# Turning a block's routing weights by a VectorE transpose and four stores instead of TensorE and ScalarE

## The chip, the core and the metric

The kernel runs on one core of a Trainium2 chip. Its time is the device time of one launch in microseconds (us). Five engines work side by side and wait for each other by semaphores: TensorE (PE: matmuls, and transposes as matmuls with the identity), VectorE (DVE), ScalarE (ACT), GpSimd (POOL) and SyncE (SP), which only issues the transfers (DMAs) here. Each engine runs its own list of instructions strictly in order.

## The reference, cut to what matters

One pre-norm transformer block over x of 32 x 256 x 128 in fp32: windowed attention with 16 heads, then a mixture of 16 experts with a shared one. What the change touches is the routing of the second half: each token gets a weight for each expert (0 for all but four), and the experts' outputs are summed by these weights.

```python
    x = x + attn(layernorm(x), ...)
    h = layernorm(x)                                   # T = 8192 tokens of 128
    scores = sigmoid(h @ gate_w.T)                     # T x 16 experts
    # two best of four groups by their two best scores + bias, then four best experts in them
    topk_weight = scores of the four / (their sum + 1e-20) * 2.5
    inter = silu(h @ gate_proj.T) * (h @ up_proj.T)    # for each expert, 64 wide
    y = sum over the four experts of topk_weight * (inter @ down_proj.T)
    shared = silu(h @ sh_gate.T) * (h @ sh_up.T) @ sh_down.T
    return x + y + shared
```

## The kernel before

The 8192 tokens are 16 blocks (STEPS) of TOK = 512 tokens, four tiles of 128 (NT = 4). Stage 1 is the attention: one body for each block, up to about 380 us of the run. Stage 2, from 397 us on, is the expert half, 16 steps d = 0 to 15 of some 22 us. Between them lies a run-up (the functions called `last`), in which the last attention block is mixed with the turning of the expert weights and the routing of blocks 0 and 1.

A step of stage 2 has nine pairs of up and down (`up(d, p)`, `down(d, p)`, p = 0 to 8; eight pairs of experts and the shared expert). The experts are two to a matmul, 64 wide each, on the 128 partitions. For each p, PE computes the gate and up projections in three matmuls of 512 columns each (lines 1560 to 1562, the inputs split into a high and a low part), ACT takes the silu (L775), DVE multiplies (`gate(d, p)`, L1105), POOL multiplies by the routing weights (`weigh(d, p)`, L618), and PE projects down three places later (`down`, L1571; the shared expert's is L1574, with 64 rows in place of 128). `up(d, p)` waits for the gate of two places before.

`weigh` needs the weights of a block as `spread`: partition = one of 128 rows of an expert pair, columns = tokens, every expert's row of 512 weights repeated on 64 partitions. SP makes this by a trip through DRAM: `store_weight(d)` writes 16 rows of 512 weights to `wt_d` (weight_scratch), and `load_spread(d)` reads them with a broadcast, two loads of 1 MB. The two `spread` buffers are the `stacks` buffers of stage 1, so the profile calls them stacks.

The weights themselves come out with tokens on the partitions. DVE computes the routing of block d + 2 in step d, in pieces between its gates, and ends with `shares(d + 2)` ahead of `gate_shared(d)`. POOL multiplies (`scale_weight(d + 2)`, L608) into `weight`, [128, 4, 16]. In step d + 1 PE turns this by four transposes into PSUM (`transpose_weights`, L1548, after up(d, 2) and the shared down), ACT copies the result to `weightT`, [16, 512] (`take_weights`, L767), and SP stores it. For block 0 the same is done in the run-up, in turn with the transposes of the expert weights through the banks ps_max (the list WEIGHT_BANKS, lines 1491 and 740). Block 0's spread load can't leave before that.

The order on every engine is written out by hand in these functions. SP's order in a step is: load_x1(d + 4), load_residual(d), store_weight(d + 1), load_spread(d + 1), store_result(d - 1).

## Time and profile before

| | us |
|---|---|
| median of three runs | 761.34 (759.34 to 766.67) |
| the profiled execution | 758.62 |
| its span, first to last instruction | 756.8 |

| engine | busy us | share of the span |
|---|---|---|
| PE | 706.9 | 93% |
| DVE | 585.8 | 77% |
| ACT | 362.4 | 48% |
| POOL | 306.4 | 40% |

The mean granted TensorE clock is 0.972 of full speed, and 1.00 in stage 2. The chain of waits, followed back from the last instruction, lies on PE for 80% of the span, on DVE for 7% and in transfers for 5%. The shares are averages over both stages; what holds in a step of stage 2 is read from its windows and timelines. An instruction's row in a timeline gives its start, its length, its engine, its line and what it writes and reads; in brackets stands how long its engine was idle before it, and what ended that.

### The profile page before, as it was taken

The page shows a single profiled execution, that of the slowest core. Times are in us where ns is not written, and L with a number is a line of the kernel's source. Part 1 is how long each engine was busy: PE and PEld are TensorE (multiplying, and loading weights), DVE is VectorE, ACT ScalarE, POOL GpSimd, SP SyncE. Part 2 cuts the span into 40 slices and gives each one's busy share as a digit, 9 for nine tenths or more (in the row PEclk, how much of TensorE's full clock was granted, in tenths as well). Part 3 has the DMA queues.
Part 4 walks back from the last instruction along what each step waited for, and adds up shares of the span by engine and source line. Part 5 has one row for each costly group of instructions (what it writes and reads, how often), then busy time and mean ns, then how long its engine had stood idle before and what let it go on. Part 6 is the DMA issues. An engine that isn't in the chain of part 4 may idle for free.

```text
span 756.8 us, 21746 instructions
## 1 busy us (share of the span) xinstructions
PE 706.9 (93%) x8499; PEld 472.2 (62%) x8499; DVE 585.8 (77%) x1741; ACT 362.4 (48%) x739; POOL 306.4 (40%) x327
## 2 busy tenths in 40 slices
PE   4597999999999999999778999999999999999997
PEld 2365666666666666666555666666666666666664
DVE  6776788888888888888577878887777888777632
ACT  2165566767776676667562332333333233333321
POOL 6410221222211222122215656566666656664543
PEclk9589899999999999999999999999999999999999
DMA  2125123333323222333118366654445666544550
GB/s 59 58 87 148 62 85 102 102 102 102 101 61 101 86 70 93 102 102 101 59 35 207 73 138 154 155 134 113 118 122 137 152 155 120 131 103 108 119 139 29
DMA packets 64837, 79.96 MB, mean 106 GB/s; under 512 B 10960, under 2 KB 38880, under 8 KB 64736
## 3 DMA queue, kind: packets, MB, share of 16 engines
q1 hardware_dynamic: 64736, 78.58, 39.9%
q8 instruction: 68, 1.11, 0.6%
q14 instruction: 33, 0.27, 0.1%
HBM read 61.00 MB, written 17.56 MB: 104 GB/s over the span
## 4 chain that ended last, share of the span: by engine, by line
PE 80%; DVE 7%; DMA 5%; ACT 4%; issue 2%; SPq 1%; POOL 1%; DVEq 0%; ACTq 0%; PEldq 0%
PE ps_c L1571 14%; PE ps_att L1356 7%; PE ps_sc L1330 6%; PE ps_max L1288 5%; PE ps_max L1560 4%; PE ps_max L1562 4%; PE ps_max L1561 4%; PE ps_sc L1306 4%; PE ps_sc L1561 4%; PE ps_sc L1562 4%; PE ps_sc L1560 4%; PE ps_a L1254 3%; ACT probs L683 3%; PE ps_c L1574 2%; PE ps_b L1247 2%
## 5 line engine op out<-in xcount | busy, mean ns | idle before, releaser
L618 POOL TENSOR_TENSOR probs<-probs,stacks 128x512 f32<-128x512 f32 x128 | 165.0, 1290 | 125.7 <-DVE probs L1105 75.4
L775 ACT ACTIVATE probs<-ps_max 128x512 f32<-128x512 f32 x144 | 86.2, 598 | 220.1 <-PE ps_max L1562 216.5
L886 DVE TENSOR_REDUCE chunkmax<-ps_max 128x16 f32<-128x512 f32 (+1 forms) x256 | 155.3, 648 | 37.9 <-PE ps_max L1269 37.8
L683 ACT ACTIVATE probs<-ps_sc 128x512 f32<-128x512 f32 x256 | 138.9, 595 | 48.6 <-PE ps_sc L1306 47.6
L1105 DVE TENSOR_TENSOR probs<-probs,ps_sc 128x512 f32<-128x512 f32 x128 | 87.3, 682 | 69.6 <-PE ps_sc L1562 26.4
L1571 PE MATMUL ps_c<-probs,wd 128*128 128x512 f32 x256 | 130.3, 592 | 1.3 <-POOL probs L618 1.3
L1560 PE MATMUL ps_max<-xh,whigh 128*128 128x512 f32 x144 | 93.7, 650 | 2.9 <-DVE probs L1105 2.1
L531 POOL TENSOR_TENSOR xres<-xin,cvec 128x512 f32<-128x512 f32 x16 | 20.6, 1287 | 141.1 <-DVE x L938 140.7
L1330 PE MATMUL ps_sc<-stacks 32*64 32x192 f16 (+2 forms) x2048 | 64.4, 232 | 9.5 <-ACT probs L683 2.7
L1356 PE MATMUL ps_att<-probs,stacks 128*32 128x192 f32 (+1 forms) x1536 | 70.2, 317 | 0.0
L1288 PE MATMUL ps_max<-hl,qdiag 32*128 32x160 f16 (+4 forms) x1024 | 50.9, 220 | 16.0 <-DVE chunkmax L886 9.7
L1330 PEld LDWEIGHTS ps_sc<-stacks 32*64 32x64 f16 x2048 | 36.6, 105 | 42.2 <-ACT probs L683 27.0
L500 POOL TENSOR_TENSOR veps<-meanvar,eps 128x4 f32<-128x4 f32 x32 | 6.4, 201 | 136.7 <-DVE meanvar L850 136.7
L1561 PE MATMUL ps_max<-xl,whigh 128*128 128x512 f32 x144 | 56.9, 395 | 0.0
L1562 PE MATMUL ps_max<-xh,wlow 128*128 128x512 f32 x144 | 56.9, 395 | 0.0
L1571 PEld LDWEIGHTS ps_c<-probs,wd 128*128 128x128 f32 x256 | 48.2, 189 | 13.6 <-POOL probs L618 1.7
L1288 PEld LDWEIGHTS ps_max<-hl,qdiag 32*128 32x128 f16 x1024 | 32.7, 95 | 35.8 <-DVE chunkmax L886 18.9
L1356 PEld LDWEIGHTS ps_att<-probs,stacks 128*32 128x32 f32 x1536 | 43.9, 111 | 16.1 <-issue 2.9
L1561 PE MATMUL ps_sc<-xl,whigh 128*128 128x512 f32 x128 | 50.8, 397 | 0.0
L1562 PE MATMUL ps_sc<-xh,wlow 128*128 128x512 f32 x128 | 50.8, 397 | 0.0
L1560 PE MATMUL ps_sc<-xh,whigh 128*128 128x512 f32 x128 | 50.5, 394 | 0.0
L1306 PE MATMUL ps_sc<-edges,repeat 64*128 64x192 bf16 (+2 forms) x576 | 49.9, 243 | 0.0
(164 smaller groups left out, 1257.1 us busy)
## 6 DMA issues: line engine op xcount, KB each, us to landing
stacks<-weight_scratch SPq DMA_DIRECT2D x32, 1024.0 KB, 10.0
stacks<-qk_scratch SPq DMA_DIRECT2D x48, 256.0 KB, 3.4
qk_scratch<-hl SPq DMA_DIRECT2D x32, 256.0 KB, 3.4
xin<-in_L_attn_x_dram SPq DMA_DIRECT2D x16, 256.0 KB, 3.1
x_scratch<-x SPq DMA_DIRECT2D x16, 256.0 KB, 2.2
xin<-x_scratch SPq DMA_DIRECT2D x16, 256.0 KB, 8.9
xres<-x_scratch SPq DMA_DIRECT2D x16, 256.0 KB, 8.9
out_dram<-result SPq DMA_DIRECT2D x16, 256.0 KB, 8.8
```

The source lines that it names most:

```text
L618: nc.gpsimd.tensor_tensor(inter[p % 3], gated[p % 2], spread[d % 2][:, p, :], ALU.mult).then_inc(inter_ready, 1)
L683: nc.scalar.activation(dst[:, :], ps_sc[s][:, 0:dst.shape[1]], ACT.Exp, scale=SCALE).then_inc(probs_ready, 1)
L775: nc.scalar.activation(silu[n % 2][rows, :], ps_max[n % 2][rows, :], ACT.Silu).then_inc(silu_ready, 1)
L886: nc.vector.tensor_reduce(chunkmax[:, 2 * pair + m, at:at + CHUNKS[h]], ps_max[m][:, 0:BANK_COLS[h]].rearrange("p (n k) -> p n k", k=KB), ...
L1105: tt(gated[p % 2], silu[n % 2], ps_sc[n % 2][:, :], ALU.mult).then_inc(gated_ready, 1)
L1288: mm(ps_max[m][:, at:at + width], qdiag[rows, b * NB + n, :, :].rearrange("p c k -> p (c k)"), hl[rows, 0, 1, b * S + key0:b * S + key0 + ...
L1330: mm(dst, qkstack[p][rows, 1, jj, q0:q0 + TB], qkstack[p][rows, 0, jj, q0:q0 + QCOLS[m]].rearrange("p (n k) -> p n k", k=TB), start=(at == ...
L1356: last = mm(ps_att[32 * x:32 * x + 32, half * S + TB * m:half * S + TB * m + QCOLS[m]].rearrange("p (n k) -> p n k", k=TB), vdiag[p][:, (b ...
L1560: mm(bank[slot][:, :], whigh[:, q, :], xh[d % 3][:, :], start=True, stop=False)
L1561: mm(bank[slot][:, :], whigh[:, q, :], xl[d % 3][:, :], start=False, stop=False)
L1562: last = mm(bank[slot][:, :], wlow[:, q, :], xh[d % 3][:, :], start=False, stop=True)
L1571: last = mm(ps_c[:, :], wd[:, p, :], inter[p % 3], start=(p == 0), stop=False)
```

## The change

`weight` is now laid out as [128, 16, 4], so that the 64 columns of a partition are (expert, tile). One DVE instruction (`transpose_weights`, a STREAM_TRANSPOSE) turns each 32x32 block of it into `weightQ`, [128, 64]. There row 32 i + q of column block b holds, for the pair (expert, tile) numbered 32 b + q, the weights of tokens 32 i to 32 i + 31 of that tile. Four stores, one for each i, bring this into the same order in `wt_d` as before: each writes 64 runs of 32 weights (128 bytes). What is gone are the four transposes of a block on PE, ACT's copy, their bank in the run-up and their waits; `transpose_y`, which uses the same bank ps_b, now waits for the earlier result alone. DVE's new instruction stands behind split_weight(6) in the run-up and behind gate(d, 1) in each step. The load of the spread waits for 64 instead of 16 increments.

```diff
--- before.py
+++ after.py
@@ -168,8 +168,8 @@
         total = sb("total", [P, NT], FP32)
         total1 = sb("total1", [P, NT], FP32)
         share = sb("share", [P, NT], FP32)
-        weight = sb("weight", [P, NT, NE], FP32)
-        weightT = [sb(f"weightT{p}", [NE, TOK], FP32) for p in range(2)]
+        weight = sb("weight", [P, NE, NT], FP32)
+        weightQ = [sb(f"weightQ{p}", [P, NE * NT], FP32) for p in range(2)]
 
         silu = [probs[n][:, :] for n in (0, 1)]
         gated = [probs[n][:, :] for n in (2, 3)]
@@ -264,8 +264,7 @@
         score_done = sem("score_done")
         share_ready = sem("share_ready")
         weight_ready = sem("weight_ready")
-        weight_tr_done = sem("weight_tr_done")
-        weightT_ready = sem("weightT_ready")
+        weightQ_ready = sem("weightQ_ready")
         weight_stored = [sem(f"weight_stored{p}") for p in range(2)]
         spread_loaded = [sem(f"spread_loaded{p}") for p in range(2)]
         route_dve = sem("route_dve")
@@ -288,9 +287,8 @@
         WEIGHT_BANKS.append((("x", 2), TOK))
         N_SPLIT = len(WEIGHT_BANKS)
         WEIGHT_BANKS += [(("down", n), 4 * P) for n in range(0, NP, 4)]
-        WEIGHT_BANKS += [(("weight",), TOK), (("sh_down",), E)]
+        WEIGHT_BANKS += [(("sh_down",), E)]
         BANK_OF_X = {1: 4, 2: N_SPLIT - 1}
-        BANK_OF_WEIGHT = N_SPLIT + 2
 
         def high_of(what):
             if what[0] == "gu":
@@ -301,8 +299,6 @@
                 return wrt[:, 0, :]
             if what[0] == "x":
                 return xh[what[1]][:, :]
-            if what[0] == "weight":
-                return weightT[0][:, :]
             if what[0] == "down":
                 return wd[:, what[1]:what[1] + 4, :].rearrange("p n k -> p (n k)")
             return wds[:, :]
@@ -422,9 +418,12 @@
 
                 if not valid(d):
                     return
-                sp.wait_ge(weightT_ready, d + 1)
+                sp.wait_ge(weightQ_ready, d + 1)
                 after(sp, spread_loaded[d % 2], 32 * (d // 2))
-                sp.dma_start(wt_d[d % 2], weightT[d % 2][:, :]).then_inc(weight_stored[d % 2], 16)
+                dst = wt_d[d % 2].rearrange("n t -> (n t)").rearrange("(b q i k) -> i q b k", b=2, q=32, i=4, k=32)
+                for i in range(4):
+                    sp.dma_start(dst[i], weightQ[d % 2][32 * i:32 * i + 32, :].rearrange("q (b k) -> q b k", b=2)
+                                 ).then_inc(weight_stored[d % 2], 16)
 
             def load_spread(d):
 
@@ -434,7 +433,7 @@
                     sp.wait_ge(pv_done, 6 * (STEPS - 1 + d))
                 else:
                     sp.wait_ge(inter_ready, NP * (d - 1))
-                sp.wait_ge(weight_stored[d % 2], 16 * (d // 2 + 1))
+                sp.wait_ge(weight_stored[d % 2], 64 * (d // 2 + 1))
                 src = wt_d[d % 2].rearrange("(n a) t -> a n t", a=2)
                 for a in range(2):
                     sp.dma_start(spread[d % 2][I * a:I * a + I, :, :], src[a].partition_broadcast(I)
@@ -604,8 +603,8 @@
                 if not valid(d):
                     return
                 pool.wait_ge(share_ready, d + 1)
-                after(pool, weight_tr_done, d)
-                nc.gpsimd.tensor_tensor(weight[:, :, :], chosen[:, :, :],
+                after(pool, weightQ_ready, d)
+                nc.gpsimd.tensor_tensor(weight[:, :, :].rearrange("p n t -> p t n"), chosen[:, :, :],
                                         share[:, :].unsqueeze(2).to_broadcast([P, NT, NE]), ALU.mult
                                         ).then_inc(weight_ready, 1)
 
@@ -736,7 +735,7 @@
             def take_weight(n):
                 dst, cols = WEIGHT_BANKS[n]
                 act.wait_ge(fw_done, n + 1)
-                rows = slice(0, {"sh_down": I, "weight": NE}.get(dst[0], P))
+                rows = slice(0, I if dst[0] == "sh_down" else P)
                 nc.scalar.copy(high_of(dst), ps_max[n % 2][rows, 0:cols]).then_inc(fw_high, 1)
 
 
@@ -757,14 +756,6 @@
                 nc.scalar.activation(silu_below, below[:, :, :], ACT.Silu)
                 nc.scalar.activation(tanh_over[:, :, :], over[:, :, :], ACT.Tanh, scale=0.5
                                      ).then_inc(score_ready, 1)
-
-            def take_weights(d):
-
-                if not valid(d):
-                    return
-                act.wait_ge(weight_tr_done, d + 1)
-                after(act, weight_stored[d % 2], 16 * (d // 2))
-                nc.scalar.copy(weightT[d % 2][:, :], ps_b[0:NE, :]).then_inc(weightT_ready, 1)
 
             def silus(d, p):
 
@@ -808,11 +799,8 @@
                 take_att(now, 1)
                 take_weight(8)
                 take_weight(9)
+                scores_of_experts(1)
                 take_weight(10)
-                act.wait_ge(fw_high, BANK_OF_WEIGHT + 1)
-                act.sem_inc(weightT_ready, 1)
-                scores_of_experts(1)
-                take_weight(11)
                 take_attn(now, 1)
 
             for i in range(-1, STEPS):
@@ -824,10 +812,8 @@
                     high_x(d + 2)
                 for p in range(NP + 1):
                     silus(d, p)
-                    if p == 2:
-                        if d > 0:
-                            take_y(d - 1)
-                        take_weights(d + 1)
+                    if p == 2 and d > 0:
+                        take_y(d - 1)
                     if p == 3:
                         scores_of_experts(d + 2)
             take_y(STEPS - 1)
@@ -1095,6 +1081,15 @@
                                         ).then_inc(route_dve, 1)
                 dve.wait_ge(route_dve, DVE_OPS * d + 24)
                 nc.vector.reciprocal(share[:, :], total1[:, :]).then_inc(share_ready, 1)
+
+            def transpose_weights(d):
+
+                if not valid(d):
+                    return
+                dve.wait_ge(weight_ready, d + 1)
+                after(dve, weight_stored[d % 2], 64 * (d // 2))
+                nc.vector.transpose(weightQ[d % 2][:, :], weight[:, :, :].rearrange("p n t -> p (n t)")
+                                    ).then_inc(weightQ_ready, 1)
 
             def gate(d, p):
 
@@ -1152,6 +1147,7 @@
                 choose_experts(0)
                 shares(0)
                 split_weight(6)
+                transpose_weights(0)
                 split_weight(7)
                 sum_logits(1)
                 clip(1)
@@ -1185,6 +1181,7 @@
                 if more:
                     tile_statistics(STEPS + d + 3, 0)
                 gate(d, 1)
+                transpose_weights(d + 1)
                 if more:
                     tile_statistics(STEPS + d + 3, 1)
                     join_statistics(STEPS + d + 3)
@@ -1485,14 +1482,6 @@
                     pe.wait_ge(xhat_ready, STEPS + 1 + what[1])
                     for t in range(NT):
                         last = nc.tensor.transpose(bank[:, t * P:(t + 1) * P], xhat[:, t, :], ident[:, :])
-                elif what[0] == "weight":
-                    pe.wait_ge(weight_ready, 1)
-                    for t in range(NT):
-                        last = nc.tensor.transpose(bank[0:NE, t * P:(t + 1) * P], weight[:, t, :], ident[:, :])
-                    last.then_inc(weight_tr_done, 1)
-                    pe.wait_ge(weight_tr_done, 1)
-                    pe.sem_inc(fw_done, 1)
-                    return
                 elif what[0] == "sh":
                     last = nc.tensor.transpose(bank[:, 0:P], wsh_raw[:, :], ident[:, :])
                 elif what[0] == "router":
@@ -1538,16 +1527,6 @@
                               start=False, stop=True, skip_group_check=True)
                 last.then_inc(logit_done, 1)
 
-            def transpose_weights(d):
-
-                if not valid(d):
-                    return
-                pe.wait_ge(weight_ready, d + 1)
-                after(pe, result_ready, d - 2)
-                for t in range(NT):
-                    last = nc.tensor.transpose(ps_b[0:NE, t * P:(t + 1) * P], weight[:, t, :], ident[:, :])
-                last.then_inc(weight_tr_done, 1)
-
             def up(d, p):
 
                 n = (NP + 1) * d + p
@@ -1577,7 +1556,7 @@
             def transpose_y(d):
 
                 pe.wait_ge(yT_ready, d + 1)
-                pe.wait_ge(weightT_ready, min(d + 3, STEPS))
+                after(pe, result_ready, d)
                 for t in range(NT):
                     last = nc.tensor.transpose(ps_b[:, t * P:(t + 1) * P], yT[:, t * P:(t + 1) * P], ident[:, :])
                 last.then_inc(y_tr_done, 1)
@@ -1622,10 +1601,9 @@
                 attend_tails(now, 1)
                 transpose_weight(8)
                 transpose_weight(9)
-                transpose_weight(10)
                 route(1)
                 transpose_att(now, 1)
-                transpose_weight(11)
+                transpose_weight(10)
                 transpose_attn(now, 1)
                 project_att(now, 1)
 
@@ -1649,8 +1627,6 @@
                         down(n // (NP + 1), n % (NP + 1))
                     if p == 1:
                         route(d + 2)
-                    if p == 2:
-                        transpose_weights(d + 1)
                     if p == 4 and d > 0:
                         transpose_y(d - 1)
                     if p == 7:
```

In a step of stage 2, PE before (p = 2: the end of up(d, 2), the shared down of the step before, the turns, the start of up(d, 3)):

```order
L1560 MATMUL ps_sc<-xh,whigh 128x512
L1561 MATMUL ps_sc<-xl,whigh 128x512
L1562 MATMUL ps_sc<-xh,wlow 128x512
L1574 MATMUL ps_c<-probs,wds 128x512
L1548 MATMUL ps_b<-ident,weight 16x128 x4
L1560 MATMUL ps_max<-xh,whigh 128x512
L1561 MATMUL ps_max<-xl,whigh 128x512
L1562 MATMUL ps_max<-xh,wlow 128x512
L1560 MATMUL ps_sc<-xh,whigh 128x512
L1561 MATMUL ps_sc<-xl,whigh 128x512
```

and after the change (with the changed kernel's line numbers):

```order
L1539 MATMUL ps_sc<-xh,whigh 128x512
L1540 MATMUL ps_sc<-xl,whigh 128x512
L1541 MATMUL ps_sc<-xh,wlow 128x512
L1553 MATMUL ps_c<-probs,wds 128x512
L1539 MATMUL ps_max<-xh,whigh 128x512
L1540 MATMUL ps_max<-xl,whigh 128x512
L1541 MATMUL ps_max<-xh,wlow 128x512
L1539 MATMUL ps_sc<-xh,whigh 128x512
L1540 MATMUL ps_sc<-xl,whigh 128x512
```

The row of four transposes from `weight` is gone, and nothing else has moved on PE; up(d, 3) follows the shared down directly.

DVE at the beginning of a step before (low_x, gate(d, 0), half of the statistics, gate(d, 1), the other half, gate(d, 2), the logits of block d + 2):

```order
L989 TENSOR_TENSOR xl<-ps_att,xh 128x512
L1105 TENSOR_TENSOR probs<-probs,ps_sc 128x512
L843 BN_STATS stats<-xin 128x6 x2
L1105 TENSOR_TENSOR probs<-probs,ps_sc 128x512
L843 BN_STATS stats<-xin 128x6 x2
L850 BN_AGGR meanvar<-stats 128x2 x4
L1105 TENSOR_TENSOR probs<-probs,ps_sc 128x512
L994 TENSOR_REDUCE logit<-ps_a 128x64
L1000 TENSOR_SCALAR below<-logit 128x64
L1001 TENSOR_SCALAR over<-logit 128x64
L1005 RECIPROCAL inverse<-below 128x64
```

and after the change:

```order
L975 TENSOR_TENSOR xl<-ps_att,xh 128x512
L1100 TENSOR_TENSOR probs<-probs,ps_sc 128x512
L829 BN_STATS stats<-xin 128x6 x2
L1100 TENSOR_TENSOR probs<-probs,ps_sc 128x512
L1091 STREAM_TRANSPOSE weightQ<-weight 128x64
L829 BN_STATS stats<-xin 128x6 x2
L836 BN_AGGR meanvar<-stats 128x2 x4
L1100 TENSOR_TENSOR probs<-probs,ps_sc 128x512
L980 TENSOR_REDUCE logit<-ps_a 128x64
L986 TENSOR_SCALAR below<-logit 128x64
L987 TENSOR_SCALAR over<-logit 128x64
L991 RECIPROCAL inverse<-below 128x64
```

One row is added, the transpose between gate(d, 1) and the second half of the statistics.

## Rows read from the trace of the kernel before

**Rows 1.** Windows view, one step: stretch, busy us by engine, clock, DMA share.

```profile
562.00:584.00 22.00, 22.00 (x90) 14.78 (x89) 17.95 (x57) 7.25 (x14) 13.79 (x13) 1.00 0.57 134
```

**Rows 2.** PE waits after step 0: waiting line <- releaser: total, times, longest us.

```profile
PE ps_b L1582 <- ACT probs L781: 0.7, 1, 0.7
```

**Rows 3.** The same view, around the start of stage 2.

```profile
PE ps_max L1560 <- DVE probs L1105: 2.1, 1, 2.1
```

**Rows 4.** Timeline of PE in step 14: start us, us, engine, line, operation.

```profile
713.99 1.12 PE L1574 MATMUL ps_c<-probs,wds 64*128 64x512 f32 x2
715.04 0.60 PE L1548 MATMUL ps_b<-ident,weight 128*16 128x128 f32 x4
...
715.72 0.40 PE L1561 MATMUL ps_max<-xl,whigh 128*128 128x512 f32 x1
```

**Rows 5.** The same view at the same place of step 15, without turns.

```profile
734.71 1.12 PE L1574 MATMUL ps_c<-probs,wds 64*128 64x512 f32 x2
...
736.11 0.39 PE L1561 MATMUL ps_max<-xl,whigh 128*128 128x512 f32 x1
```

**Rows 6.** Tile view of weight, PE: count, least, median, longest ns.

```profile
L1548 PE MATMUL ps_b<-ident,weight x60: 272/273/277, 403.8 to 715.4; 128*16 128x128 f32 x60
```

**Rows 7.** Timeline of PE: before up(7, 1), and before up(8, 1).

```profile
555.48 1.02 PE L1571 MATMUL ps_c<-probs,wd 128*128 128x512 f32 x2
...
577.51 1.02 PE L1571 MATMUL ps_c<-probs,wd 128*128 128x512 f32 x2
578.00 0.76 PE L1560 MATMUL ps_max<-xh,whigh 128*128 128x512 f32 x1
```

**Rows 8.** Timeline of DVE: gate_shared(7), gate(8, 1), gate(8, 2).

```profile
577.16 0.69 DVE L1112 TENSOR_TENSOR probs<-probs,ps_max 64x512 f32<-64x512 f32 x1
...
580.01 0.69 DVE L1105 TENSOR_TENSOR probs<-probs,ps_sc 128x512 f32<-128x512 f32 x1 [0.44 <-ACT probs L775]
...
583.15 0.69 DVE L1105 TENSOR_TENSOR probs<-probs,ps_sc 128x512 f32<-128x512 f32 x1 [1.51 <-ACT probs L775]
```

**Rows 9.** Timeline of POOL: scale_weight(9), weigh(8, 0), weigh(8, 1).

```profile
577.21 0.29 POOL L608 TENSOR_TENSOR weight<-chosen,share 128x64 f32<-128x64 f32 x1 [0.83 <-DVE share L1097]
579.30 1.28 POOL L618 TENSOR_TENSOR probs<-probs,stacks 128x512 f32<-128x512 f32 x1 [1.80 <-DVE probs L1105]
580.92 1.28 POOL L618 TENSOR_TENSOR probs<-probs,stacks 128x512 f32<-128x512 f32 x1 [0.34 <-PE ps_c L1571]
```

**Rows 10.** Timeline, first weights: split_weight(6), scale_weight(0), store, load.

```profile
388.25 0.66 DVE L977 TENSOR_TENSOR wlow<-ps_max,whigh 128x512 fp32r<-128x512 f32 x1
388.42 0.29 POOL L608 TENSOR_TENSOR weight<-chosen,share 128x64 f32<-128x64 f32 x1 [6.68 <-DVE share L1097]
...
391.74 0.32 SPq L427 DMA_DIRECT2D weight_scratch<-weightT  x1
...
393.37 1.30 SPq L440 DMA_DIRECT2D stacks<-weight_scratch  x2
```

**Rows 11.** Timeline of POOL, first weigh of stage 2.

```profile
405.77 2.49 POOL L618 TENSOR_TENSOR probs<-probs,stacks 128x512 f32<-128x512 f32 x2 [5.20 <-DMA stacks<-weight_scratch]
```

**Rows 12.** Timeline of DVE, gate(0, 2), which waited for it.

```profile
407.17 0.69 DVE L1105 TENSOR_TENSOR probs<-probs,ps_sc 128x512 f32<-128x512 f32 x1 [3.76 <-POOL probs L618]
```

**Rows 13.** Timeline of the SP queue, store and load in step 7.

```profile
563.25 0.32 SPq L427 DMA_DIRECT2D weight_scratch<-weightT  x1
565.00 1.27 SPq L440 DMA_DIRECT2D stacks<-weight_scratch  x2
```

**Rows 14.** Line view of L915, the 32x32 transpose that the kernel has.

```profile
L915 DVE STREAM_TRANSPOSE rowmaxT<-rowmax x32: 211/213/214, 30.8 to 364.9; 128x32 f16<-128x32 f16 x32
```

**Rows 15.** Line view of L427, landing of the weight store.

```profile
DMA to landing us min/median/max: 1.6/1.6/2.5
```

**Rows 16.** DMA view: KB each, median us to landing.

```profile
stacks<-weight_scratch SPq DMA_DIRECT2D x32, 1024.0 KB, 10.0
...
max_scratch<-rowmaxT SPq DMA_DIRECT2D x32, 8.0 KB, 1.4
```

## The prediction

> **What bounds the kernel now.** I read the table of the 40 slices first, then the windows, the waits, the chain of waits and last the timelines. Only stage 2 and its run-up turn routing weights, so the attention stage (up to about 380 us) stays as it is. In the windows view a step of stage 2 fills TensorE (PE) completely: 22.00 of 22.00 us, at a granted clock of 1.00, while VectorE (DVE) works 17.95, GpSimd (POOL) 13.79 and ScalarE (ACT) 7.25 us [rows 1]. The waits say the same: after step 0, PE stands still once, for 0.7 us, at the very end [rows 2]. So a PE instruction taken out of a step shortens the step, as long as nobody becomes late in its place. The start of stage 2 is different. There PE waits 2.1 us for a gate on DVE [rows 3]. Followed back, POOL's first weigh began at 405.77 after 5.20 us of waiting for the spread load [rows 11], and gate(0, 2) on DVE began at 407.17 after 3.76 us of waiting for that weigh [rows 12]. What ends last there is a transfer, which hangs on the weights of block 0.
>
> **PE: four turns less in each step.** The turns of a block are four matmuls of 273 ns each; 60 of them are in the tile view, 15 blocks, beside four in the run-up [rows 6]. The trace tells what they cost without any theory of overlapping. In step 14, from the shared down-projection (713.99) to the second matmul of the next up (715.72) takes 1.73 us, turns included [rows 4]. In step 15, which has no further block to route, the same stretch without turns takes 736.11 - 734.71 = 1.40 us [rows 5]. So they cost **0.33 us**, though the timeline shows them as 0.60 us long: part of that time passes between the two kinds of matmul in any case. The bounds are 0.33 and 0.60; I take 0.33, which is measured at the same place. The turns of step 0 stand ahead of the wait for the spread load and are absorbed by it, so 14 steps count: 14 x 0.33 = **4.6 us** (upper bound 14 x 0.60 = 8.4).
>
> **DVE: one transpose more in each step.** The kernel has such a transpose already, in f16 and half as wide: 213 ns at all 32 places [rows 14]. For 128x64 in fp32 I take 0.25 us; the bounds are 0.21 and, if it had to stand behind a POOL operation, 1.3 more, the length of a weigh [rows 9]. It stands behind gate(d, 1), which ended at 580.70, and ahead of gate(d, 2), before which DVE was idle for 1.51 us [rows 8]. It finds its input ready: scale_weight(9) ran at 577.21, three microseconds ahead [rows 9]. And it begins at 580.70, 0.2 us before POOL starts its next weigh at 580.92. Cost on the path: nothing; it is covered by those 1.51 us, which hold even the upper bound as far as gate(d, 2) is concerned. If the cover were gone, each step would pay up to 0.25 us, 3.5 us in all. Queued behind it are the second half of the statistics and gate(d, 2).
>
> **What is late next.** In each step DVE is busy almost without pause from gate(d, 3) to gate_shared(d). The latter ended at 577.85 [rows 8], and up(8, 1) is recorded at 578.00, behind a matmul shown until 578.53 [rows 7]: a margin of at most 0.5 us. But nothing is removed between up(d, 3), which releases gate(d, 3), and up(d + 1, 1), which waits. Both ends of that stretch move together, so the margin stays.
>
> **ACT, POOL and SP.** ACT loses a copy of a step in which it works 7.25 of 22 us: nothing. POOL writes the same 64 columns in strides of four; it took 0.29 us and 1.80 us of waiting followed: nothing [rows 9]. SP issues four stores instead of one, behind load_x1 and load_residual and ahead of load_spread. In step 7 the store went at 563.25 and the load at 565.00 [rows 13]; with 10.0 us to landing [rows 16] it was there at 575.0, 4.3 us ahead of the weigh at 579.30 [rows 9]. A step is 577.51 - 555.48 = 22.03 us long [rows 7]. After the change the store can go behind gate(7, 1) and the transpose, so 22.0 us before 580.95, at 558.9: another 4.3 us of room. Four stores may take some 10 us before anybody sees them: nothing.
>
> **The start of stage 2.** Here the store is on the path. Before: weight written by 388.71, four turns, ACT's copy, store at 391.74, load at 393.37 [rows 10], weigh at 405.77. After: split_weight(6) ended at 388.91 [rows 10], the transpose ends at about 389.2, and the first store goes at 389.25. The trace has no store of 128-byte runs. Issuing costs 0.32 us as for the old store, or 0.65 as for each of the two loads [rows 10]; landing takes 1.6 us as for the old store (2.5 at most) [rows 15], or 1.4 as for a store of 8 KB [rows 16]. Best case: 389.25 + 3 x 0.32 + 1.4 = 391.6, the load 1.75 us earlier. Worst case: 389.25 + 3 x 0.65 + 2.5 = 393.7, 0.35 us later. I take the middle for issuing (0.5) and 1.6 for landing, since the rows are near in size: 392.35, the load at 392.4, **1.0 us** earlier. Everything from the weigh to 424 us hangs on it and moves with it; PE's run-up gets shorter as well, but it waits for the load anyway. split_weight(7) comes 0.25 us later, likewise covered.
> Those 8 KB stores are where a rule speaks against the change. The Trainium skill (DMA: Bandwidth & Descriptors, section on the anatomy of one DMA) puts some 2.0 us of fixed time on each transfer, whatever its size. This trace shows 1.6 at the median for one; whether four overlap, it does not show. One behind the other they would take 8.0 us by that page, the load would leave at 397.3 instead of 393.4, and the sum would be a gain of 4.6 - 3.9 = 0.7 us instead of 5.6.
>
> **The sum.** 4.6 + 1.0 = 5.6 us. The profiled execution took 758.62 us, span 756.8: 753.0 after. The median of the three runs is 761.34, 2.7 above it, so **755.7** on that footing.
>
> **The rivals.**
> A. The turns are worth their recorded 0.60 us. For it: they are on a PE that is full. Against it: step 15, unless its up waits there for something of its own. 8.4 + 1.0 = 9.4 us: 751.9.
> B. The stores eat the start, by the worst case above: 4.6 - 0.35 = 4.3 us: 757.0. For it: four issues, short runs. Against it: 2.5 us is the longest landing of 16, and their median is 1.6 [rows 15].
> C. Slower: the four stores of block 0 land one behind the other, 2.5 us each [rows 15]. The load leaves at 389.25 + 10.0 = 399.3, 5.9 us later; with the 4.6 us gained in the steps that is 1.3 us slower: 762.6. It decides from 4.1 + 4.6 = 8.7 us for the four (4.1 is 393.37 - 389.25), 2.2 us each. Against it: two loads go out within 1.30 us without waiting for one another [rows 10].
> D. The change does not shorten the step: DVE with its small margin sets the pace, so PE waits at up(d, 1) instead of turning. Gain 1.0 us: 760.3. For it: the margin of 0.5 us. Against it: 4 us of idle time in DVE's step [rows 1].
>
> **How the numbers follow.** Forecast 0.60, A 0.14, B 0.14, D 0.07, C 0.05. The measurement can tell about 1% from no change, which is 7.6 us: faster means below 753.7, slower above 769.0. The forecast lies 2.0 us above that border, and the three runs of before lie 7.3 us apart, so I give a quarter of the forecast's chance to faster, and nearly all of A's: 0.28. Slower by 1% needs C and more, or a disturbed comparison: 0.05. The rest, 0.67, is no change. The range reaches from 750.0 (A, with a median 2 us low) to 760.5 (D), leaving out C and half the tails.
>
> **What would show it.** In the changed profile: PE still full in the steps, and the stretch from L1574's successor to the next up 1.40 us long in every step, so steps of 21.7 us (right), or 21.4 (A), or 22.0 with PE waiting for DVE at up(d, 1) (D). The transpose at 0.25 us with an idle gap before gate(d, 2). The first spread load issued at 392.4 and the first weigh at 404.8. I would be wrong if the transpose ran into POOL's weighs and took over 2 us, if the load left after 393.4, or if the steps shortened by another amount than 0.33.

## The result, and the profile after

The changed kernel takes **759.25 us** in the median of 20 runs (753.55 to 762.65); the kernel before, run beside it, 763.32 us (20 runs, 758.19 to 766.67). The ratio is 0.9938, with a 95% interval of 0.9918 to 0.9958: a gain of 4.7 us at this length, 3.2 to 6.3. Forecast were 5.6 us and 755.7, in a range from 750.0 to 760.5.

The profiled execution of the changed kernel is its slowest of the 20 (762.65 us, span 760.9), while that of before lies under all but one of before's 20 runs (758.62, span 756.8). So the two spans must not be subtracted. Where do they part? The table of slices shows a part of it (busy tenths of PE, then the granted clock), and the view of the attention stage's own transpose, the one of [rows 14], another:

```profile
PE   4497999999999999999788899999999999999997
...
PEclk9589899999999999999978999999999999999999
...
L901 DVE STREAM_TRANSPOSE rowmaxT<-rowmax x32: 211/211/213, 31.1 to 371.5; 128x32 f16<-128x32 f16 x32
```

Before has a clock of 9 in all slices from the sixth on; here there are a 7 and an 8 in the 21st and 22nd, which reach from 380 to 418 us (the run-up and the beginning of stage 2). But the last transpose of the attention stage starts at 371.5 already, against 364.9 [rows 14]: 6.6 us of the distance arise in the attention stage, where the change touches nothing. split_weight(6), which ended at 388.91 before, ends at 398.20, and in a second profile of the same kernel (changed_again, below) at 390.98. All that follows is therefore measured from that instruction:

| | end of split_weight(6) to first load | first load to first weigh | first weigh to the end | together |
|---|---|---|---|---|
| before | 4.46 | 12.40 | 351.03 | 367.89 |
| changed | 3.01 | 12.40 | 347.29 | 362.70 |
| gain | 1.45 | 0 | 3.74 | 5.2 |

Together 5.2 us, inside the interval of the ratio. (The page gives a span to 0.1 us, so the last two columns hold to 0.05.)

**A step.** PE's timeline in the changed kernel (start us, us, engine, line, operation): the down-projections ahead of up(d, 1) in two successive steps, which answer to [rows 7], and below them the shared down with the next up directly behind it, which answers to [rows 4]:

```profile
561.71 1.02 PE L1550 MATMUL ps_c<-probs,wd 128*128 128x512 f32 x2
...
583.48 1.02 PE L1550 MATMUL ps_c<-probs,wd 128*128 128x512 f32 x2
...
588.96 1.12 PE L1553 MATMUL ps_c<-probs,wds 64*128 64x512 f32 x2
590.01 0.50 PE L1539 MATMUL ps_max<-xh,whigh 128*128 128x512 f32 x1
590.36 0.39 PE L1540 MATMUL ps_max<-xl,whigh 128*128 128x512 f32 x1
```

From the shared down to the second matmul of the next up pass 590.36 - 588.96 = 1.40 us, as forecast and as in [rows 5]. A step is 583.48 - 561.71 = 21.77 us long, against 22.03: 0.26 less, not 0.33. PE still has no pause in it; the windows row answers to [rows 1], the waits (from 430 us on) to [rows 2]. The wait of 0.2 us stands at up(1, 1), and before has it too (the last row), though [rows 2] leaves it out:

```profile
562.00:584.00 22.00, 22.00 (x88) 14.62 (x86) 18.32 (x59) 6.72 (x13) 13.80 (x13) 1.00 0.57 134
```

```profile
PE ps_b L1561 <- ACT probs L772: 0.7, 1, 0.7
...
PE ps_max L1539 <- DVE probs L1107: 0.2, 1, 0.2
...
PE ps_max L1560 <- DVE probs L1112: 0.2, 1, 0.2
```

DVE works 18.32 us of the 22 (17.95 before). The new instruction on it, in the same timeline form:

```profile
585.98 0.69 DVE L1100 TENSOR_TENSOR probs<-probs,ps_sc 128x512 f32<-128x512 f32 x1 [0.50 <-ACT probs L766]
586.59 0.24 DVE L1091 STREAM_TRANSPOSE weightQ<-weight 128x64 f32<-128x64 f32 x1
586.75 0.44 DVE L829 BATCH_NORM_STATS2 stats<-xin 128x6 f32<-128x128 f32 x2
587.37 0.38 DVE L836 BATCH_NORM_AGGREGATE meanvar<-stats 128x2 f32<-128x6 f32 x4 [0.17 <-DVE stats L829]
589.12 0.69 DVE L1100 TENSOR_TENSOR probs<-probs,ps_sc 128x512 f32<-128x512 f32 x1 [1.38 <-ACT probs L766]
```

It takes 0.24 us, and the idle gap ahead of gate(d, 2) falls from 1.51 us [rows 8] to 1.38. It was paid for out of that gap.

**The start of stage 2.** POOL writes weight, DVE turns it, SP stores it four times and then sends the two loads (SPq is SyncE's issue of a DMA; a row joins neighbouring instructions of one line, xN):

```profile
397.70 0.31 POOL L607 TENSOR_TENSOR weight<-chosen,share 128x64 f32<-128x64 f32 x1 [8.01 <-DVE share L1083]
398.11 0.23 DVE L1091 STREAM_TRANSPOSE weightQ<-weight 128x64 f32<-128x64 f32 x1
...
398.37 1.74 SPq L425 DMA_DIRECT2D weight_scratch<-weightQ  x4
...
401.21 1.30 SPq L439 DMA_DIRECT2D stacks<-weight_scratch  x2
...
413.61 2.51 POOL L617 TENSOR_TENSOR probs<-probs,stacks 128x512 f32<-128x512 f32 x2 [4.82 <-DMA stacks<-weight_scratch]
```

The same two lines over the whole kernel, in the view of the tile weightQ (duration ns least/median/longest, first and last start), with the landing of the stores:

```profile
L425 SPq DMA_DIRECT2D weight_scratch<-weightQ x64: 302/421/1394, 398.4 to 718.5; - x64
L1091 DVE STREAM_TRANSPOSE weightQ<-weight x16: 233/238/239, 398.1 to 716.9; 128x64 f32<-128x64 f32 x16
...
DMA to landing us min/median/max: 1.3/1.5/3.4
```

From the first store's issue to the load pass 401.21 - 398.37 = 2.84 us: three issues of about 0.43, one landing of 1.5. The stores overlap: one behind the other, four landings of 1.5 would take 6.0.

### The profile page after: what moved, and what is told of

The parts are those of the page before. It is cut to its first block, busy times and chain, and to the rows that moved or that the text cites. A ratio compares the mean times of both kernels' runs of the same rounds, so it can differ in the third digit from the quotient of the medians.

```text
span 760.9 us, 21649 instructions
## 1 busy us (share of the span) xinstructions
PE 708.3 (93%) x8435; PEld 471.6 (62%) x8435; DVE 588.8 (77%) x1757; ACT 354.2 (47%) x723; POOL 306.4 (40%) x327
## 4 chain that ended last, share of the span: by engine, by line
PE 77%; DVE 8%; DMA 6%; ACT 3%; issue 2%; SPq 2%; POOL 1%; DVEq 0%; ACTq 0%
PE ps_c L1550 14%; PE ps_att L1353 7%; PE ps_sc L1327 6%; PE ps_max L1539 5%; PE ps_max L1285 4%; PE ps_max L1541 4%; PE ps_max L1540 4%; PE ps_sc L1303 4%; PE ps_sc L1541 4%; PE ps_sc L1540 4%; PE ps_sc L1539 4%; DVE chunkmax L872 3%; PE ps_a L1251 3%; DMA xin<-in_L_attn_x_dram 2%; PE ps_c L1553 2%; ACT probs L682 2%
## 5 line engine op out<-in xcount | busy, mean ns | idle before, releaser
L1539 PEld LDWEIGHTS ps_max<-xh,whigh 128*128 128x128 f32 x144 | 27.5, 191 | 38.0 <-issue 36.4
```

What stands on the lines that cost most here:

```text
L1539: mm(bank[slot][:, :], whigh[:, q, :], xh[d % 3][:, :], start=True, stop=False)
```

## Experiments

Times are medians, with the ratio to the kernel before, which ran in each of the four sets (medians 764.6, 763.5, 763.1 and 761.6 us). The first set holds changed again, turns back, turns late and five more on DVE; the second start as before, two stores, first in pieces and one turn; the third 24 more on DVE and the two wide kernels; the last turn and pieces. This table is the study in the stretches used above; "to load" is from the end of split_weight(6) to the first spread load, "rest" from the first weigh to the end, and "step" from one up(d, 1) to the next in a regular step. shared_wide has no stretches, since its profiled execution is the longest of its 12 (766.67 us).

| kernel | to load | load to weigh | rest | together | step | median | ratio, 95% interval |
|---|---|---|---|---|---|---|---|
| before | 4.46 | 12.40 | 351.03 | 367.89 | 22.03 | | |
| changed again | 3.03 | 12.43 | 348.56 | 364.02 | 21.77 | 757.53 | 0.9888 (0.9847 to 0.9930) |
| turns back | 3.02 | 12.57 | 351.04 | 366.63 | 22.03 | 760.74 | 0.9955 (0.9928 to 0.9981) |
| turns late | 3.02 | 12.61 | 353.63 | 369.26 | 22.23 | 765.65 | 1.0008 (0.9981 to 1.0036) |
| five more on DVE | 3.02 | 12.47 | 347.33 | 362.82 | 21.77 | 756.24 | 0.9885 (0.9848 to 0.9923) |
| 24 more on DVE | 3.01 | 12.57 | 360.32 | 375.90 | 22.74 | 770.17 | 1.0096 (1.0067 to 1.0125) |
| start as before | 4.46 | 12.56 | 347.29 | 364.31 | 21.77 | 759.00 | 0.9955 (0.9927 to 0.9982) |
| two stores | 2.75 | 12.49 | 347.38 | 362.62 | 21.77 | 757.05 | 0.9925 (0.9892 to 0.9958) |
| first in pieces | 3.01 | 7.94 | 349.32 | 360.27 | 21.77 | 753.75 | 0.9888 (0.9851 to 0.9924) |
| one turn | 3.02 | 12.64 | 346.28 | 361.94 | 21.69 | 755.76 | 0.9912 (0.9879 to 0.9945) |
| shared wide | | | | | | 761.90 | 0.9982 (0.9953 to 1.0011) |
| wide and pieces | 3.02 | 7.93 | 354.69 | 365.64 | 22.2 | 759.70 | 0.9952 (0.9927 to 0.9976) |
| turn and pieces | 3.03 | 7.93 | 348.62 | 359.58 | 21.69 | 750.69 | 0.9862 (0.9825 to 0.9899) |

The stretches don't hold the whole difference of the medians. In the first comparison the medians lie 4.1 us apart, 1.1 less than the stretches; in all eleven experiments with stretches the kernel lies better against its set's before than they say, by 0.3 (turns late) to 3.3 us (five more on DVE: 8.4 against 5.1). The stretches leave out all that lies ahead of the end of split_weight(6), which comes between 388.9 and 398.2 us in these profiles. Whether the change has a part in that, no run shows; causes below are read from the stretches.

**changed_again**: the changed kernel as it is, in one set with the next three.

> The changed kernel once more, as it is, so that the others stand beside it on the same chip. Theory (turns off TensorE, and an earlier first load): the stretch from up(d, 2) to up(d, 3) is 2.65 us again (2.98 before), the first spread load leaves 3.0 us after split_weight(6) ends (4.5 before), and the time is 4 to 5.5 us below before. Rival (the slower stage 1 of its first profile belongs to the change): the time until split_weight(6) ends is again some 9 us above the 388.9 us of before; by the theory it is not.

757.53 us, and split_weight(6) ends at 390.98, 2.1 us later than before's and not 9, so the rival is refuted as it stands. The stretches of the profile repeat but for the rest, which is 1.3 us longer. 1.2 us of that are step 0 (25.00 us from up(0, 1) to up(1, 1), against 23.80), and in its middle stands a window with 0.75 of the clock.

```profile
414.00:420.00 6.00, 4.46 (x11) 2.90 (x12) 5.83 (x19) 0.60 (x1) 4.08 (x4) 0.75 1.06 218
```

**turns_back** puts four turns on PE where they were; what they write is overwritten by the next matmul into the bank.

```diff
+            def turns(d, shown):
+                after(pe, result_ready, shown)
+                for t in range(NT):
+                    nc.tensor.transpose(ps_b[0:NE, t * P:(t + 1) * P], bias[:, :], ident[:, :])
...
+                    if p == 2 and d < STEPS - 1:
+                        turns(d, d - 1)
```

> The changed kernel, with four turns put back on TensorE in the place of the old ones (behind the shared down at p = 2, steps 0 to 14, same shapes, of a constant tile, into the same bank, read by nobody). DVE's transpose and the four stores stay, ACT's copy stays away. Theory: up(d, 2) to up(d, 3) takes 2.98 us again, 0.33 more, and the time is 3.5 to 4.6 us above the changed kernel, so 1 to 1.5 us below before (what the earlier first load gives). Rival 1 (the gain came from ACT's copy and the waits that are gone): the time is that of the changed kernel. Rival 2 (the turns cost their recorded 0.60 us): 8.4 us above the changed kernel.

The rest is 351.04 us, that of before (351.03), though the start stays the new one, and ACT's copy and the waits stay away. So the 3.74 us of the steps are PE's turns and nothing else. The rows (timeline of PE) show how much of their length counts:

```profile
583.99 1.12 PE L1559 MATMUL ps_c<-probs,wds 64*128 64x512 f32 x2
585.04 0.60 PE L1534 MATMUL ps_b<-ident,bias 128*16 128x128 f32 x4
585.40 0.48 PE L1545 MATMUL ps_max<-xh,whigh 128*128 128x512 f32 x1
585.72 0.39 PE L1546 MATMUL ps_max<-xl,whigh 128*128 128x512 f32 x1
```

585.72 - 583.99 = 1.73 us, against 1.40 without them: recorded 0.60, paid 0.33.

**turns_late**: the same four turns, called with `if p == 6`, behind a down-projection of 128 rows.

> The same four turns, but behind the down at p = 6, where a matmul with 128 rows stands ahead of them and not the shared down with its 64. Theory (the old place hid part of their cost, because some 0.1 us passes there between the kinds of matmul in any case): up(d, 6) to up(d, 7) goes from 2.26 to 2.69 us, as at the two places where the kernel turns other things (p = 4 and 7), up(d, 2) to up(d, 3) stays at 2.65, and the time is 14 x 0.43 = 6.0 us above the changed kernel, about 1 us above before. Rival (four turns of this size cost 0.33 wherever they stand): 4.6 us above the changed kernel, no later than before.

Here the two places stand in one kernel, a step's p = 5 without turns and p = 6 with them (timeline of PE):

```profile
594.02 1.02 PE L1556 MATMUL ps_c<-probs,wd 128*128 128x512 f32 x2
...
595.12 0.39 PE L1546 MATMUL ps_max<-xl,whigh 128*128 128x512 f32 x1
...
596.29 1.02 PE L1556 MATMUL ps_c<-probs,wd 128*128 128x512 f32 x2
597.14 0.60 PE L1534 MATMUL ps_b<-ident,bias 128*16 128x128 f32 x4
...
597.82 0.39 PE L1546 MATMUL ps_max<-xl,whigh 128*128 128x512 f32 x1
```

1.10 us become 1.53: 0.43 for turns that read 0.60 here too. Behind the 64-row shared down they cost 0.33. The stretch there is already 0.30 longer without them (1.40 against 1.10), and that they fill a part of it fits the 0.10 between the two prices; it is argued, not shown. The steps are 0.46 us longer each than the changed kernel's, 22.23 against 21.77. The median is 8.1 us above that of changed_again, the rest 5.1 (against changed_again) to 6.3 us longer (against the first profile of the changed kernel); what the median has beyond that is not explained.

**dve_five_more** and **dve_24_more** add transposes to DVE behind the new one; nobody reads them.

```diff
+                if d > 0:
+                    for n in range(5):
+                        nc.vector.transpose(spare[:, n, :], ident[:, 0:64])
```

> The changed kernel with five more 32x32-block transposes of the same size on VectorE in each step 1 to 15, right behind the real one (of a constant tile into a tile that nobody reads): 6 x 0.24 = 1.4 us there in place of 0.24. Theory (the transpose is covered by DVE's idle time of 1.5 us ahead of gate(d, 2)): the idle time shrinks to about 0.3 us and the time is that of the changed kernel within 1 us. Rival (DVE's margin at up(d, 1) is what sets the step): 1.2 us in each of 14 steps, up to 17 us slower.

> The changed kernel with 24 more transposes on VectorE in each step 1 to 15 (constant tile, read by nobody). Five more took 0.71 us, so 24 take about 3.1. Theory (the cover is 1.4 us ahead of gate(d, 2) and about 1.0 ahead of gate(d, 3); behind it lies a margin of some 0.3 us at up(d + 1, 1)): 3.1 - 1.4 - 1.0 - 0.3 = 0.4 us of waiting on PE in each of 13 steps with routing, 5 us above the changed kernel, and the waits of PE name DVE's shared gate. Rival (DVE has 4 us of idle time in a step, all of it cover): the time of the changed kernel.

Five cost nothing: rest 347.33, steps 21.77, gap ahead of gate(d, 2) down to 0.75 (timeline of DVE):

```profile
578.91 0.24 DVE L1093 STREAM_TRANSPOSE weightQ<-weight 128x64 f32<-128x64 f32 x1
579.07 0.71 DVE L1097 STREAM_TRANSPOSE spare<-ident 128x64 f32<-128x64 f32 x5
...
581.45 0.69 DVE L1105 TENSOR_TENSOR probs<-probs,ps_sc 128x512 f32<-128x512 f32 x1 [0.75 <-ACT probs L768]
```

With 24 the gap is gone, and PE begins to wait at up(d, 1), in 12 steps (two of the 24 kernel's DVE rows, the second with the row of changed_again for the same three operations below it, then its row in the waits of PE, from 430 us on):

```profile
587.98 3.12 DVE L1097 STREAM_TRANSPOSE spare<-ident 128x64 f32<-128x64 f32 x24
...
595.75 2.27 DVE L1014 TENSOR_TENSOR pair_sums<-choice 128x48 f32<-128x48 f32 x3
...
588.21 1.15 DVE L1012 TENSOR_TENSOR pair_sums<-choice 128x48 f32<-128x48 f32 x3
```

```profile
PE ps_max L1544 <- DVE probs L1112: 4.8, 12, 0.4
```

The expected 5 us were far too few: the rest is 11.8 us longer than in changed_again (13.0 than in the changed kernel's first profile), the median 12.6 above that of changed_again. A step is 0.97 us longer, 0.65 of it in the stretch to up(d, 1) (2.90 instead of 2.25), of which the profile names 0.4 as a wait, 0.24 between up(d, 5) and up(d, 6), where it names none, and 0.1 between up(d, 8) and the next up(d, 0). The expectation reckoned with 3.1 us more on DVE. But DVE's own operations, which the transposes delay, also last longer: the three that make pair_sums take 2.27 us instead of 1.15, the second of them 1.07 instead of 0.19, beside POOL's weigh of 595.59 (1.28) and its xhat of 596.83 (1.04). So DVE got some 4.2 us more, and how the 0.97 divides between the transposes and this lengthening no run separates. Rival D names a real limit, reached with these 4.2 us, not with 0.24.

**start_as_before** gives back the old way for block 0 alone: four turns on PE, ACT's copy, one store.

```diff
+                if d == 0:
+                    sp.dma_start(wt_d[0], weightT[:, :]).then_inc(weight_stored[0], 16)
+                    return
...
+                elif what[0] == "weight":
+                    pe.wait_ge(weight_ready, 1)
+                    for t in range(NT):
+                        last = nc.tensor.transpose(bank[0:NE, t * P:(t + 1) * P], weight[:, :, t], ident[:, :])
```

> The changed kernel, but block 0 goes the old way in the run-up (turned by TensorE in its bank, copied by ScalarE, one store); all later blocks go the new way. Theory (the start gives 1.45 us, the steps the rest): the first spread load leaves 4.4 us after split_weight(6) ends instead of 3.0, the steps are 21.77 us long as in the changed kernel, and the time is 1 to 2 us above the changed kernel. Rival (the start gives nothing, since run-up and PE catch up in step 0): the same time as the changed kernel.

4.46 us from the end of split_weight(6) to the load, as before, and a rest of 347.29, that of the changed kernel. (The medians, 759.00 here and 759.25 for the changed kernel, are from different sets; the 1.45 us are too few to be read from them.) The two halves of the change are thus apart: 1.45 at the start, 3.74 in the steps. The issues:

```profile
394.92 0.32 SPq L429 DMA_DIRECT2D weight_scratch<-weightT  x1
396.55 1.30 SPq L447 DMA_DIRECT2D stacks<-weight_scratch  x2
```

From the store to the load it took 1.63 us here and 2.84 with four stores, so the four cost 1.2 us at this place; what they save is the way to the first store: issued 0.17 us after split_weight(6) ends, instead of 2.84.

**two_stores** writes the turned block in two stores of 16 KB.

```diff
-                for i in range(4):
-                    sp.dma_start(dst[i], weightQ[d % 2][32 * i:32 * i + 32, :].rearrange("q (b k) -> q b k", b=2)
+                for b in range(2):
+                    sp.dma_start(dst[b], weightQ[d % 2][:, 32 * b:32 * b + 32]).then_inc(weight_stored[d % 2], 16)
```

> The changed kernel with the weights stored in two DMAs of 16 KB (one for each block of 32 columns, 128 partitions each, the same runs of 128 bytes) instead of four of 8 KB. Theory (at the start the path holds three issues of 0.45 us and one landing, and landings overlap): two issues less, the first spread load leaves 0.9 us earlier, 2.1 us after split_weight(6); 0.5 to 1 us faster, at the edge of what can be measured, and read from the timeline. Rival (the number of 128-byte runs sets the landing): the last landing is longer by as much and the load leaves as in the changed kernel.

```profile
394.26 1.11 SPq L425 DMA_DIRECT2D weight_scratch<-weightQ  x2
396.83 1.31 SPq L438 DMA_DIRECT2D stacks<-weight_scratch  x2
```

The load comes 2.57 us after the first store, 0.27 better than with four, so neither the 0.9 of the theory nor the nothing of the rival. Each issue takes 0.56 instead of 0.43, and from the last store's issue to the load pass 2.0 us instead of 1.5. The rival (the last landing is longer by what is saved) is the nearer of the two; whether the bytes or the number of 128-byte runs lengthen it is open, since both double, and this trace has no landing times for these stores.

**first_in_pieces** loads block 0's spread weights in four parts, so that p = 0 and 1 need only the first two.

```diff
+                pieces = [(slice(0, 2), spread_first), (slice(2, NP), spread_loaded[0])] if d == 0 else [
+                    (slice(0, NP), spread_loaded[d % 2])]
+                for n, loaded in pieces:
+                    for a in range(2):
+                        sp.dma_start(spread[d % 2][I * a:I * a + I, n, :], src[a][n].partition_broadcast(I)
+                                     ).then_inc(loaded, 16)
```

> The changed kernel with block 0's spread load in two pieces: expert pairs 0 and 1 first (0.5 MB), on a semaphore of their own, then the other six; weigh(0, 0) waits for the first piece, weigh(0, 2) for the second. Theory (step 0 hangs on the whole 2 MB load of 12.4 us): weigh(0, 0) starts right behind gate(0, 0), PE's and DVE's waits in step 0 shrink, and all later work comes 2 to 3 us earlier. Rival (step 0 is bound by DVE's chain of routing and gates, whenever it begins): less than 1 us.

```profile
396.14 2.59 SPq L443 DMA_DIRECT2D stacks<-weight_scratch  x4
```

```profile
404.08 1.27 POOL L623 TENSOR_TENSOR probs<-probs,stacks 128x512 f32<-128x512 f32 x1 [0.37 <-DVE probs L1106]
```

The first weigh comes 7.94 us after the load instead of 12.40, and it now waits for DVE (the bracket), not for the transfer. Of these 4.5 us the sum keeps 2.4; the rest of step 0 has other waits, one of them 0.61 us of weigh(0, 2) for the second piece. The median is 753.75.

**one_turn**: a single turn of 128 columns in the place of the four.

```diff
+                nc.tensor.transpose(ps_b[0:NE, 0:P], bias[:, :], ident[:, :])
```

> The changed kernel with one of the four turns put back on TensorE behind the shared down (read by nobody). With no turn there, the stretch up(d, 2) to up(d, 3) is 2.65 us and four later stretches of the step are 0.02 us longer each (2.27 for 2.25); with four turns it is 2.98. Theory (the change from the 64-row shared down to the up costs some 0.1 us that a turn hides, and a turn also puts the later matmuls back to their shorter pace): 2.65 us with one turn as with none, and the later stretches at 2.25, so steps of 21.70 us and 1 us less time than the changed kernel. Rival (turns cost 0.08 us each, linearly, and the pace belongs to something else): 2.73 us, and steps of 21.8 us or more.

```profile
581.88 1.12 PE L1558 MATMUL ps_c<-probs,wds 64*128 64x512 f32 x2
582.93 0.28 PE L1533 MATMUL ps_b<-ident,bias 128*16 128x128 f32 x1
582.97 0.48 PE L1544 MATMUL ps_max<-xh,whigh 128*128 128x512 f32 x1
583.28 0.39 PE L1545 MATMUL ps_max<-xl,whigh 128*128 128x512 f32 x1
```

(One of its eight runs took 957.58 us; the median doesn't feel it.) 583.28 - 581.88 = 1.40: one turn costs nothing there. And the step is 21.69, **shorter** than without it (21.77), because the five stretches that follow have before's pace again (2.24, 2.68, 2.25, 2.25, 2.68 instead of 2.27, 2.70, 2.27, 2.26, 2.69). These are the 0.08 us a step which the forecast lacks.

**shared_wide** and **wide_and_pieces** make the shared down 128 rows deep, with zeros below, to take away the 0.30 us of the 64-row form.

```diff
-        wds = sb("wds", [I, E], FP32)
+        wds = sb("wds", [P, E], FP32)
...
-                    last = mm(ps_c[:, :], wds[:, :], inter[p % 3][0:I, :], start=False, stop=True)
+                    last = mm(ps_c[:, :], wds[:, :], inter[p % 3], start=False, stop=True)
```

> The changed kernel with the shared expert's down-projection made as wide as the others: its weights get 64 more rows of zeros, so that the matmul uses 128 rows in place of 64. Theory (the 64-row matmul and the change between the kinds make the stretch up(d, 2) to up(d, 3) 0.40 us longer than an ordinary one and the four stretches behind it 0.02 each; the turns hid in part of this): the stretch becomes 2.25 us, the later ones 2.25 and 2.68, steps 21.3 us, and the time 6 to 7 us below the changed kernel. Rival (a matmul with half the rows is no slower; the 0.40 us are a wait for ScalarE or VectorE at this place): 2.65 us as before, no gain.

> Both together: the shared down-projection with 128 rows, and block 0's spread load in two pieces. Theory: the gains lie in different stretches (every step; step 0 alone) and add up: 6 to 7 us and 2.5 us below the changed kernel, about 1.8% below before. Rival (VectorE's margin is used up by the shorter steps): PE waits for DVE's shared gate in each step, and the gain is less than 6 us in all.

The stretch did shrink, from 2.65 to 2.25 us between one up's second matmul and the next one's, yet a step is 22.2 us long and the rest 354.69. shared_wide alone took 761.9 us, ratio 0.9982 (0.9953 to 1.0011). What came late is read from wide_and_pieces. By its stretches it is 2.9 us slower than the changed kernel (365.64 against 362.70), where 6 to 7 and 2.5 us less were expected, and PE waits for DVE's shared gate: its rival was right. Waits of PE from 440 us on, then DVE and POOL at the same moment:

```profile
PE ps_max L1547 <- DVE probs L1115: 4.7, 12, 0.4
```

```profile
585.79 1.34 DVE L994 TENSOR_SCALAR below<-logit 128x64 f32<-128x64 f32 x1
587.05 1.08 DVE L995 TENSOR_SCALAR over<-logit 128x64 f32<-128x64 f32 x1
```

```profile
585.78 1.30 POOL L625 TENSOR_TENSOR probs<-probs,stacks 128x512 f32<-128x512 f32 x1 [0.62 <-PE ps_c L1561]
587.03 1.04 POOL L508 TENSOR_TENSOR xcent<-xin,meanvar 128x512 f32<-128x512 f32 x1
```

The two operations on 64 columns take as long as POOL's weigh and xcent, beside which they stand. In the changed kernel (the profile of changed_again) they run in 0.20 and 0.19 us, just ahead of or across the start of POOL's weigh at 584.30:

```profile
584.12 0.20 DVE L986 TENSOR_SCALAR below<-logit 128x64 f32<-128x64 f32 x1
584.23 0.19 DVE L987 TENSOR_SCALAR over<-logit 128x64 f32<-128x64 f32 x1
```

There the first of them was 0.18 us ahead of POOL's weigh; here, with PE's stretch shortened, the two begin together, and DVE loses 2.0 us a step on them (1.34 + 1.08 against 0.20 + 0.19). The score behind them lasts 1.26 us instead of 0.23, beside another weigh, while choice and pair_sums get shorter by 1.0 together. In all, these operations take 5.2 us of a step instead of 3.1. The Trainium skill (SBUF — State Buffer, section "Who interferes with whom") says that a tensor_scalar of DVE can take the port pair that it shares with GpSimd, and that whoever has it blocks the other for a whole instruction; by that rule each of the two would last as long as its neighbour on POOL, and the trace agrees: 1.34 beside 1.30, 1.08 beside 1.04. The new transpose shows nothing of the kind: 233 to 239 ns in all 16 places, and 24 of them in 3.12 us beside two weighs, the rate of five in 0.71.

**turn_and_pieces** joins what had helped: one_turn and first_in_pieces.

> The changed kernel with the two edits that gained by themselves: one turn kept behind the shared down (nobody reads it), and block 0's spread load in two pieces. Theory (one acts in steps 1 to 13, the other in step 0): steps of 21.68 us, step 0 of 21.1 us instead of 23.7, together 1.2 + 2.6 = 3.8 us below the changed kernel. Rival (the pace of DVE and POOL that step 0 leaves behind decides, as with the wide shared expert): steps longer than 21.77 us with PE waiting for DVE, and no more gain than the pieces alone.

750.69 us (748.81 to 757.22), ratio 0.9862 (0.9825 to 0.9899): the lowest time of the study, 1.4% below before, its parts as the two kernels had them singly (load to weigh 7.93, step 21.69). Of the expected 3.8 us below the changed kernel, 3.1 are there in the stretches. That it beats the changed kernel rests on the stretches, 359.58 us against 362.70; against the ratio of the first comparison, 0.9938 (0.9918 to 0.9958), it is clear of it, against that of changed_again it is not.

## Why the prediction was right

**The bound.** PE full in every step, no wait after step 0: it held before and holds after. Only for this reason does a removed instruction shorten the step.

**PE's turns: right in kind, 0.9 us too much.** 0.33 us at their place is what all runs show (1.73 against 1.40, removed or put back). The term 14 x 0.33 = 4.6 failed in one point: it took the other stretches of the step as unchanged. They grew by 0.08 us together, so 0.26 a step was left, 14 x 0.26 = 3.6, and 3.74 with the ends, where the stretches grew less. The prediction named this itself as a sign of being wrong ("if the steps shortened by another amount than 0.33"); it has come about, in the size and not in the mechanism. The row for it stood in reach: step 15, from which the 0.33 was read, has the longer stretches too (2.27, 2.70, 2.27, 2.26 against 2.25, 2.68, 2.25, 2.25 in the steps with turns), and only its first stretch was used. Rival A (0.60) is refuted by turns_back.

**DVE's transpose: right.** 0.238 us measured, 0.25 taken; its input was ready, it ended at 586.83, 0.06 us before POOL's next weigh started, and the gap of 1.51 us took it up. Five more were covered as well. Rival D did not come true; its margin of some tenths was left untouched because both its ends moved together, as argued, and dve_24_more and wide_and_pieces show what it costs where they do not.

**ACT, POOL and SP: right, nothing seen.** Scaling into strides of four takes 0.31 us on POOL instead of 0.29 [rows 9], no named wait follows from it.

**The start: right in kind, too small.** Forecast 1.0, measured 1.45 (4.46 to 3.01; start_as_before isolates it). Of the 0.45, 0.17 is the first store, issued 0.17 us after split_weight(6) ended, not 0.34; the rest is the stores themselves, 2.84 us to the load instead of 3 x 0.5 + 1.6 = 3.1. The absolute times that the prediction gave as signs (load by 393.4) can't be compared, since split_weight(6) ended 9.3 us later in this profile; counted from it, the load was forecast at 3.5 and came at 3.0. Rival B (issues of 0.65, landing 2.5) is out, and so is C, the four landing one behind the other. The Trainium skill (DMA: Bandwidth & Descriptors, the anatomy of one DMA) describes some 2.0 us fixed for each transfer on GpSimd's path; the prediction took it for these stores too, which SyncE issues. As a price of one it is near what SP's stores show, 1.5 at the median; as a sum over four it would be 8.0 us, and the trace has 2.84.

**The sum.** 5.6 forecast, 5.2 in the profile, 4.7 (3.2 to 6.3) in the runs: a term 0.9 too large and one 0.45 too small, and it is luck that one makes up for half of the other. Of the 3.6 us between 755.7 and 759.25, 2.0 are the footing: the forecast stood on a median of 761.34, and 20 runs of before gave 763.32. The other 1.5 are the gain itself, 4.1 us between the two medians instead of 5.6.

## What to carry to other kernels

Take the price of an instruction on a full engine from two stretches of the trace that differ in it alone, and then compare the **whole** loop body in both, not only the place of the cut: here the place gave 0.33 and the body 0.26. (Two whole bodies must be of the same kind: step 15 has no routing, and only its common stretches compare.) A chain across three engines and a store (turn, copy, store) can be worth replacing with more, smaller transfers if their issues overlap with their landings; count from the first issue to the consumer. And before shortening a stretch on the bound engine, look which pairs of DVE and GpSimd operations it will slide on top of one another.

## What the hardware showed

- Four turns of 16x128 cost 0.33 us behind a matmul of 64 rows, 0.43 behind one of 128 rows, and one alone cost nothing; all read as 0.60 and 0.28 us.
- The shared down of 64 rows makes the stretch to the next up 0.30 us longer than one of 128 rows does (1.40 against 1.10), though it moves half the rows.
- With no turn between that down and the next up, the following stretches of the step are 0.01 to 0.02 us longer each, up to the fifth. One turn, four turns, or a shared down of 128 rows takes that away. **Its cause is open**: step 14 shows it in some profiles and not in others, step 1 of the changed kernel's first profile doesn't (2.25, 2.68, 2.25), and no engine's wait stands beside it.
- A transpose of 128x64 in fp32 takes DVE 0.24 us alone and 0.13 us in a row of its kind.
- TENSOR_SCALAR of 128x64 in fp32 goes from 0.20 to 1.34 us beside a GpSimd operation of 1.30, and the second TENSOR_TENSOR for pair_sums from 0.19 to 1.07 beside one of 1.04.
